# A fused decoder layer on one core: maximum rounds half a batch earlier, key products ahead of the last values, heads copied by ScalarE

## Chip, cores and metric

The kernel runs on one core of one Trainium2 chip. The metric is the device time of one execution in microseconds, the median over timed runs.

## What is computed

A pre-norm decoder layer over 16 batches of 56 tokens, 128 wide, all in float32:

```
x = x + self_attention(layernorm(x))            # 16 heads of 8, keys: the 56 tokens
x = x + cross_attention(layernorm(x), ctx, bias) # 16 heads of 8, keys: 1500 rows of ctx per batch
x = x + moe(layernorm(x))                       # 32 experts of width 64, top 4, and a shared expert
```

Cross attention is where most of the work is: keys and values are `ctx @ Wk.T` and `ctx @ Wv.T`, scores are `q.k / sqrt(8)` plus a bias per key, then softmax over 1500 keys and the weighted sum of the values. Each softmax needs the maximum over the 1500 keys, for each query and head.

## The kernel before

**Stages.** Weights and x are loaded, self attention runs over the 16 batches, then the cross attention over the 16 batches in a software pipeline of iterations (`iteration(r, c)`, batch i = 3r + c), then the router and the experts. Operands are split in two fp16 parts, and a product is three matmuls (`split_matmul`, L356 to L358). Iterations -1, 0 and 13 to 16 are written out; iterations 1 to 12 are a hardware loop of four passes over three iterations, in each engine's own program.

**One iteration** has six blocks, `for d in range(ND)`. Batch i has 12 key tiles of 125 keys, two for each block. In block d TensorE computes the scores of tile 2d (`scores`, L914) into two banks, `stb[0]` and `stb[1]`; multiplies the probabilities of the two tiles before with the values (`pv_tile`, L797 and L800); computes the scores of tile 2d + 1; then a small use of the bank `misc`, a maximum round, and a large use of `misc`. ScalarE makes each half of a score tile into probabilities (`exponential`, L1197). The two score banks are used again by the next tile, so the second half of a tile waits for the exponential of the second half of the tile before.

**Maximum rounds.** The maxima come from a second computation of the scores, without the row that subtracts the maximum: `max_round` (L891) makes eight matmuls on 31 rows and 64 columns, which fill four banks, and VectorE takes the maxima (`take_round`, L1523) in two reduces. A batch has six rounds; `round_of(d)` says which round of which batch stands in block d: rounds 2 to 5 of batch i + 1 in blocks 0 to 3, rounds 0 and 1 of batch i + 2 in blocks 4 and 5. After round 5 VectorE writes `mcol`; TensorE folds it in a small product (`mt`, L947), ScalarE copies it to `mrow` (L1217) and a DMA on ScalarE's queue (L1222) puts it into row 127 of the queries `qsb` of batch i + 1. The first scores of the next iteration wait for that DMA (`mrow_in`).

**The bank misc** is used in the order of the list `MISC`, each use waiting until the one before has been read (`misc_read`). Small uses are `sel` (block 1, `pick_heads` L807: the head sums of batch i - 1), `tr` (block 2, L944: transpose of the normalized tokens `tok`), `mt` (block 4). Large uses are V0, V1, V2 (values of batch i + 2, blocks 0 to 2) and K0, K1, K2 (keys of batch i + 3, blocks 3 to 5). After `sel`, VectorE's `normalize` (L1413 to L1419) reads misc in three operations and writes `tok`; the next large use waits for the last of them. ScalarE reads the large uses (`take_values` L1137, `take_keys` L1133).

**Other engines.** POOL splits keys (`split_keys`, L598 and L602) and the context (`split_first` L578, `split_second` L588) into two parts; SP's queue, at the start of iteration i, waits for the scores of batch i - 1 and issues for batch i + 2 two bias rows (L450), three queries (L458), three key copies (L467), then the transposes of the context of batch i + 4 (L435) and the load of that of batch i + 6 (L420). The first round of a batch waits for all of its keys and queries.

**Expert stage.** For each pair of experts and each half of the tokens TensorE makes three products of `hidden`, the `gates` product (L1003) of `pairsel` and `gt` on 64 rows, three more of `hidden`, and `down` (L1018). VectorE multiplies and splits (L1616, L1588, L1621).

## Time and profile before

| | us |
|---|---|
| median of 3 timed runs | 589.97 (588.26 to 594.99) |
| the profiled execution, device time | 591.73 |
| its span, first to last instruction | 590.0 |
| TensorE matmuls busy | 498.9 (85%) |
| VectorE busy | 383.1 (65%) |
| ScalarE busy | 333.8 (57%) |
| POOL busy | 270.5 (46%) |
| mean granted clock of TensorE | 0.901 of full speed |

L914 is line 914 of the kernel. PE is TensorE's matmul, PEld its weight load, DVE VectorE, ACT ScalarE, POOL GpSimd, SP SyncE; a q behind an engine's name is its queue. "idle before" is the time an engine stood still just ahead of the work, and behind the arrow is what ended it.

### The profile page before, as it was taken

The page shows a single profiled execution, that of the slowest core. Times are in us where ns is not written, and L with a number is a line of the kernel's source. Part 1 is how long each engine was busy: PE and PEld are TensorE (multiplying, and loading weights), DVE is VectorE, ACT ScalarE, POOL GpSimd, SP SyncE. Part 2 cuts the span into 40 slices and gives each one's busy share as a digit, 9 for nine tenths or more (in the row PEclk, how much of TensorE's full clock was granted, in tenths as well). Part 3 has the DMA queues.
Part 4 walks back from the last instruction along what each step waited for, and adds up shares of the span by engine and source line. Part 5 has one row for each costly group of instructions (what it writes and reads, how often), then busy time and mean ns, then how long its engine had stood idle before and what let it go on. Part 6 is the DMA issues. An engine that isn't in the chain of part 4 may idle for free.

```text
span 590.0 us, 17600 instructions
## 1 busy us (share of the span) xinstructions
PE 498.9 (85%) x6656; PEld 312.8 (53%) x6656; DVE 383.1 (65%) x615; ACT 333.8 (57%) x699; POOL 270.5 (46%) x201
## 2 busy tenths in 40 slices
PE   2644988768889999799979999799999887789996
PEld 1224666514556656466646656566666665334442
DVE  6972433579657767477656767477777942588885
ACT  2330165432767777477756777567776684345553
POOL 7895530074672683464570863634440040035540
PEclk9865599956789999899989999799999998599999
DMA  4147184015447547626655347516302210012101
GB/s 135 70 109 149 44 168 123 2 71 143 119 127 149 136 141 133 164 63 169 153 129 157 103 114 168 155 29 152 99 15 87 56 42 14 1 28 54 40 0 32
DMA packets 89117, 56.66 MB, mean 96 GB/s; under 512 B 74910, under 2 KB 80342, under 8 KB 89046
## 3 DMA queue, kind: packets, MB, share of 16 engines
q1 hardware_dynamic: 88390, 55.54, 37.4%
q8 instruction: 58, 0.95, 0.7%
q10 hardware_dynamic: 656, 0.06, 0.1%
q14 instruction: 13, 0.11, 0.1%
HBM read 17.01 MB, written 0.46 MB: 30 GB/s over the span
## 4 chain that ended last, share of the span: by engine, by line
PE 64%; DVE 13%; issue 10%; DMA 7%; ACT 2%; POOL 2%; SPq 1%; ACTq 0%; DVEq 0%; POOLq 0%
PE ps L914 15%; PE ps L797 10%; PE ps L356 8%; DMA qsb<-mrow 6%; PE ps L358 6%; PE ps L357 6%; DVE mx L1523 4%; PE ps L891 3%; PE ps L1018 3%; PE ps L800 3%; PE ps L773 3%; PE ps L807 2%; DVE xn L1305 2%; PE ps L1003 2%; SPq L444 1%
## 5 line engine op out<-in xcount | busy, mean ns | idle before, releaser
L1523 DVE TENSOR_REDUCE mx<-ps 120x2 f32<-120x1000 f32 x192 | 220.8, 1193 | 92.5 <-PE ps L891 92.4
L914 PE MATMUL ps<-qsb,ks 128*125 128x224 f16 x768 | 129.7, 279 | 21.6 <-issue 12.3
L1197 ACT ACTIVATE p<-ps 125x448 f32<-125x448 f32 x256 | 126.2, 540 | 31.5 <-PE ps L914 29.1
L598 POOL TENSOR_TENSOR k<-k,zero 128x500 f16<-128x500 f32 x45 | 45.9, 1020 | 142.9 <-ACT k L1133 142.9
L914 PEld LDWEIGHTS ps<-qsb,ks 128*125 128x125 f16 x768 | 78.8, 140 | 59.5 <-issue 23.7
L1197 ACT ACTIVATE wnat<-ps 125x448 f32<-125x448 f32 x128 | 63.9, 541 | 9.3 <-PE ps L914 9.2
L797 PE MATMUL ps<-p,v 125*27 125x168 f32 x1152 | 67.5, 316 | 0.4 <-DVE v L1429 0.4
L578 POOL TENSOR_TENSOR ch<-ctx,zero 128x1536 f16<-128x1536 f32 x16 | 44.9, 2807 | 23.1 <-issue 19.7
L602 POOL TENSOR_TENSOR k<-k 128x500 f16<-128x500 f32 x45 | 52.8, 1174 | 3.5
L588 POOL TENSOR_TENSOR ch<-ctx,ch 128x1536 f16<-128x1536 f32 x16 | 52.0, 3252 | 3.2 <-DMA ct<-ch 3.1
L1137 ACT ACTIVATE v<-ps 125x512 f32<-125x512 f32 x48 | 28.9, 601 | 43.3 <-PE ps L358 43.1
L891 PE MATMUL ps<-ks,qsb 31*64 31x500 f16 (+1 forms) x768 | 46.0, 417 | 4.8 <-DVE mx L1523 4.6
L356 PE MATMUL ps<-wt,ct 128*125 128x128 f16 x192 | 41.4, 246 | 5.7 <-DVE tok L1419 4.9
L669 POOL TENSOR_TENSOR ks<-ks,zero 128x384 f16<-128x384 f32 x17 | 19.6, 1155 | 51.5 <-PE ps L1018 40.2
L1133 ACT ACTIVATE k<-ps 128x500 f32<-128x500 f32 x45 | 26.4, 587 | 28.7 <-PE ps L358 28.7
L800 PE MATMUL ps<-p,v 125*9 125x56 f32 x1152 | 41.1, 215 | 0.0
L567 POOL TENSOR_TENSOR rstd<-veps,mhalf 128x4 f32<-128x4 f32 (+1 forms) x6 | 5.7, 949 | 73.3 <-DVE veps L1298 73.3
L357 PE MATMUL ps<-wt,ct 128*125 128x128 f16 x192 | 39.1, 234 | 0.0
L358 PE MATMUL ps<-wt,ct 128*125 128x128 f16 x192 | 38.9, 234 | 0.0
L356 PEld LDWEIGHTS ps<-wt,ct 128*125 128x125 f16 x192 | 28.6, 149 | 19.1 <-DVE tok L1419 8.7
L800 PEld LDWEIGHTS ps<-p,v 125*9 125x9 f32 x1152 | 32.4, 92 | 7.5
L1255 ACT ACTIVATE v<-ps 128x448 f32<-128x448 f32 x34 | 18.4, 544 | 27.5 <-PE ps L358 27.5
(184 smaller groups left out, 897.0 us busy)
## 6 DMA issues: line engine op xcount, KB each, us to landing
ks<-k SPq DMA_DIRECT2D x48, 375.0 KB
ctx<-in_ctx SPq DMA_DIRECT2D x16, 750.0 KB
ks<-in_L_ffn_W SPq DMA_DIRECT2D x48, 64.0 KB, 2.0
qsb<-late SPq DMA_DIRECT2D x32, 56.0 KB, 3.5
ks<-brow SPq DMA_DIRECT2D x32, 46.9 KB
qs<-late SPq DMA_DIRECT2D x8, 168.0 KB, 3.6
qsb<-qd SPq DMA_DIRECT2D x16, 56.0 KB, 2.6
qs<-qd SPq DMA_DIRECT2D x4, 168.0 KB, 3.8
```

The source lines that it names most:

```text
L356: nc.tensor.matmul(out, a1, b1, start=True, stop=False)
L357: nc.tensor.matmul(out, a1, b2, start=False, stop=False)
L358: return nc.tensor.matmul(out, a2, b1, start=False, stop=True)
L588: nc.gpsimd.tensor_tensor(ch[:, 1], ctx[b % 2][:], ch[:, 0], ALU.subtract).then_inc(ch_ok[1], 1)
L598: nc.gpsimd.tensor_tensor(k12[:, 0, cols], k32[:, cols], zero[:].rearrange("p a b -> p (a b)").to_broadcast([128, CH]), ALU.add).then_inc( ...
L602: nc.gpsimd.tensor_tensor(k12[:, 1, cols], k32[:, cols], k12[:, 0, cols], ALU.subtract).then_inc(k_ok, 1)
L797: mm(obank[32 * quad:32 * quad + 27, 0:168], vt[0:keys, 27 * quad:27 * quad + 27], pt[0:keys, 168 * quad:168 * quad + 168], start=first, s ...
L800: done = mm(obank[32 * quad:32 * quad + 9, 168:224], vt[0:keys, 108 + 9 * quad:117 + 9 * quad], pt[0:keys, 672 + S * quad:672 + S * quad + ...
L891: last = mm(mxb[64 * upper:64 * upper + width, j, 0:CH], qsb[n][32 * j:32 * j + 31].rearrange("p h q -> p (h q)")[:, first:first + width], ...
L914: last = mm(stb[half][0:KP, 224 * (g % 2):224 * (g % 2) + 224], ks[c % 3][:, g, KP * s:KP * s + KP], qsb[c % 3][:, HG * g:HG * g + HG].rea ...
L1197: A(p[s % 3][0:KP, 448 * half:448 * half + 448], stb[half][0:KP, 0:448], ACT.Exp, scale=SCALE).then_inc(exp_done, 1)
L1523: V.tensor_reduce(mx[:, h:h + 2, k // 2], mxb[0:120, 2 * pair:2 * pair + 2, 0:CH], axis=AX.X, op=ALU.max).then_inc(mx_read, 1)
```

## The change

Rounds 3 to 5 of batch i + 1 stand in blocks 0 to 2 and rounds 0 to 2 of batch i + 2 in blocks 3 to 5; `mt` moves to block 3 and `tr` to block 4; the keys stand in blocks 2 to 4 and V2 in block 5. Round and small use are issued ahead of the odd scores. ScalarE copies misc after `sel` to a new tile `heads`, and `normalize` reads it there, after the round. The DMA of the maximum row is issued between the two odd exponentials. SP issues keys, queries, bias rows in this order. `pairsel` and `gt` get 128 rows, the upper 64 of them zero.

```
--- before.py
+++ after.py
@@ -66,12 +66,12 @@
 
 
 
-MISC = ["V0", "sel", "V1", "tr", "V2", "K0", "mt", "K1", "K2"]
-SMALL = {1: "sel", 2: "tr", 4: "mt"}
-LARGE = ["V0", "V1", "V2", "K0", "K1", "K2"]
-
-
-TAIL = {(B - 2, "V0"): "out", (B - 2, "K0"): "norm", (B - 1, "V0"): "logits"}
+MISC = ["V0", "sel", "V1", "K0", "mt", "K1", "tr", "K2", "V2"]
+SMALL = {1: "sel", 3: "mt", 4: "tr"}
+LARGE = ["V0", "V1", "K0", "K1", "K2", "V2"]
+
+
+TAIL = {(B - 2, "V0"): "out", (B - 2, "K1"): "norm", (B - 1, "V0"): "logits"}
 OFFSET = {"K": 3, "V": 2, "s": -1, "t": -1, "m": 1}
 BEFORE_LOOP = 2 * B + 1
 
@@ -121,7 +121,7 @@
 
 def round_of(d):
 
-    return (1, d + 2) if d < 4 else (2, d - 4)
+    return (1, d + 3) if d < 3 else (2, d - 3)
 
 
 def self_uses(j):
@@ -159,7 +159,7 @@
         zero = sb("zero", [128, 1, 1], F32)
         ones_h = sb("ones_h", [128, 128], F16)
         before = sb("before", [128, 128], F16)
-        pairsel = sb("pairsel", [64, NP, 2, HE], F16)
+        pairsel = sb("pairsel", [128, NP, 2, HE], F16)
         expert_no = sb("expert_no", [128, NE], F32)
 
         wnat = sb("wnat", [128, 8, 128], F32)
@@ -214,6 +214,7 @@
         osb = sb("osb", [128, 224], F32)
         rec = sb("rec", [S, 4, 4], F32)
         tok = sb("tok", [128, D], F32)
+        heads = sb("heads", [S, 144], F32)
 
 
         flat = lambda t, d, n, o=0: t[:].rearrange("p a b -> p (a b)").bitcast(d)[:, o:o + n]
@@ -238,7 +239,7 @@
         rrec = flat(ctx[1], F32, TT, 1104)
         chosen_h = flat(ks[2], F16, 224).rearrange("p (j e) -> p j e", e=NE)
         gpair = flat(ks[2], F16, 448, 256).rearrange("p (j e) -> p j e", e=64)
-        gt = flat(ks[2], F16, T, 1024)[0:64]
+        gt = flat(ks[2], F16, T, 1024)
 
         ps = stack.enter_context(nc.psum_tensor("ps", [128, 8, 512], F32))
         sbank = [ps[:, 0:2, :], ps[:, 2:4, :]]
@@ -295,6 +296,7 @@
         misc_done = sem("misc_done")
         misc_read = sem("misc_read")
         norm_step = sem("norm_step")
+        tok_ok = sem("tok_ok")
         o_psum = sem("o_psum")
         xb_ok = sem("xb_ok")
         x_ok = sem("x_ok")
@@ -491,9 +493,9 @@
 
                 if i + 2 < B:
                     sp.wait_ge(st_done, scores_before(0, i))
+                    key_stacks(i + 2)
+                    load_queries(i + 2)
                     bias_rows(i + 2)
-                    load_queries(i + 2)
-                    key_stacks(i + 2)
                 transpose_ctx(i + 4)
                 load_ctx(i + 6)
                 if i == B - 2:
@@ -655,10 +657,9 @@
             split_first(3)
             split_second(3)
             for i in range(-1, B - 3):
-                split_keys(i + 3, 0)
+                for j in range(3):
+                    split_keys(i + 3, j)
                 split_first(i + 5)
-                split_keys(i + 3, 1)
-                split_keys(i + 3, 2)
                 split_second(i + 5)
 
             def split_experts(u, n, it):
@@ -941,6 +942,7 @@
                     pe.wait_ge(o_read, B + 3 * r + c)
                     pick_heads()
                 elif use == "tr":
+                    pe.wait_ge(tok_ok, 3 * r + c + 1)
                     tr(misc[:, 0:128], tok[:], ident[:]).then_inc(misc_done, 1)
                 elif use == "mt":
                     pe.wait_ge(mcol_ok, 3 * r + c + 2)
@@ -953,19 +955,19 @@
                     for t in (2 * d - 2, 2 * d - 1):
                         if live(r, c if t >= 0 else c - 1):
                             pv_tile(r, c if t >= 0 else c - 1, t % KT)
-                    if live(r, c):
-                        scores(r, c, 2 * d + 1)
-                    if d in SMALL:
-                        small_use(r, c, SMALL[d])
                     off, k = round_of(d)
                     if live(r, c + off):
                         max_round(r, c, off, k)
+                    if d in SMALL:
+                        small_use(r, c, SMALL[d])
+                    if live(r, c):
+                        scores(r, c, 2 * d + 1)
                     large_use(r, c, LARGE[d])
 
             for use in ("K0", "K1", "K2"):
                 large_use(0, -2, use)
             pe.wait_ge(q2_ok, 3)
-            for k in range(2):
+            for k in range(ROUNDS // 2):
                 max_round(0, -2, 2, k)
             transpose_norm(1, 1, 1, xt_psum)
             pe.wait_ge(xt2_ok, 4)
@@ -1206,9 +1208,11 @@
                     if d == 0 and live(r, c - 1):
                         act.wait_ge(pv_done, B + KT * i)
                         A(osb[:], obank[:, 0:224], ACT.Copy).then_inc(o_read, 1)
-                    if live(r, c):
-                        exponential(r, c, 2 * d + 1, 0)
                     use = SMALL.get(d)
+                    if use == "sel" and used(r, c, use):
+                        act.wait_ge(misc_done, misc_index(r, c, use) + 1)
+                        act.wait_ge(tok_ok, 3 * r + c)
+                        A(heads[:], misc[0:S, 0:144], ACT.Copy).then_inc(misc_read, 1)
                     if use == "tr" and used(r, c, use):
                         act.wait_ge(misc_done, misc_index(r, c, use) + 1)
                         A(attn[:, bass.ds(S * (i - 1), S)], misc[:, 0:S], ACT.Copy).then_inc(misc_read, 1)
@@ -1216,11 +1220,13 @@
                         act.wait_ge(misc_done, misc_index(r, c, use) + 1)
                         A(mrow[:], misc[0:H, 0:S], ACT.Copy, scale=1.0 / BIG).then_inc(misc_read, 1)
                     if live(r, c):
-                        exponential(r, c, 2 * d + 1, 1)
+                        exponential(r, c, 2 * d + 1, 0)
                     if use == "mt" and used(r, c, use):
                         act.wait_ge(misc_read, misc_index(r, c, use) + 1)
                         act.dma_start(qsb[(c + 1) % 3][MAXROW:MAXROW + 1], mrow[:]
                                       ).then_inc(mrow_in[(c + 1) % 3], 16)
+                    if live(r, c):
+                        exponential(r, c, 2 * d + 1, 1)
                     use = LARGE[d]
                     if used(r, c, use):
                         if tail(r, c, use) == "norm":
@@ -1395,8 +1401,8 @@
             for n in range(2):
                 V.memset(p[n][:], 0.0)
             V.memset(mcol[:], 0.0)
-            V.tensor_tensor(fold[:], ident[0:120, 0:S], ident[0:120, 64:120], ALU.add)
-            V.memset(tok[:], 0.0).then_inc(clear_ok, 1)
+            V.memset(tok[:], 0.0).then_inc(tok_ok, 1)
+            V.tensor_tensor(fold[:], ident[0:120, 0:S], ident[0:120, 64:120], ALU.add).then_inc(clear_ok, 1)
             self_maxima(0)
             with dve.Fori(1, B // 4, 1) as r:
                 self_maxima(r)
@@ -1406,10 +1412,10 @@
             V.tensor_tensor(xs[:], xs[:], bp[:].rearrange("p (o d) -> p o d", o=1).to_broadcast([128, TT, D]),
                             ALU.add).then_inc(xb_ok, 1)
 
-            def normalize(batches):
-
-
-                part = misc[0:S, 0:144].rearrange("p (k a e) -> p k a e", k=4, a=4)
+            def normalize(batches, src, done):
+
+
+                part = src[0:S, 0:144].rearrange("p (k a e) -> p k a e", k=4, a=4)
                 V.reciprocal(rec[:], part[:, :, :, HD]).then_inc(norm_step, 1)
                 dve.wait_ge(norm_step, batches + 1)
 
@@ -1418,7 +1424,7 @@
                                 ALU.mult)
                 V.tensor_tensor(tok[0:S, 96:128].rearrange("p (a e) -> p a e", a=4), part[:, 3, :, 0:HD],
                                 rec[:, 3, :].rearrange("p (a o) -> p a o", o=1).to_broadcast([S, 4, HD]),
-                                ALU.mult).then_inc(misc_read, 1)
+                                ALU.mult).then_inc(done, 1)
 
             def self_step(r, c):
                 j, k = 2 * r + c, c % 2
@@ -1431,7 +1437,7 @@
                                     bv[:].rearrange("p (h e) -> p h e", h=H), ALU.add).then_inc(vself_ok, 1)
                 if self_live(r, c - 2):
                     dve.wait_ge(misc_done, self_index(r, c, "sel") + 1)
-                    normalize(j - 2)
+                    normalize(j - 2, misc, misc_read)
 
                 if isinstance(r, int) and j == OUT_STEP:
                     dve.wait_ge(xb_ok, 1)
@@ -1531,12 +1537,12 @@
             def iteration(r, c):
                 i = 3 * r + c
                 for d in range(ND):
-                    if SMALL.get(d) == "sel" and used(r, c, "sel"):
-                        dve.wait_ge(misc_done, misc_index(r, c, "sel") + 1)
-                        normalize(B + i - 1)
                     off, k = round_of(d)
                     if live(r, c + off):
                         take_round(r, c, off, k)
+                    if SMALL.get(d) == "sel" and used(r, c, "sel"):
+                        dve.wait_ge(misc_read, misc_index(r, c, "sel") + 1)
+                        normalize(B + i - 1, heads, tok_ok)
                     use = LARGE[d]
                     if tail(r, c, use) == "out":
                         dve.wait_ge(misc_done, misc_index(r, c, use) + 1)
@@ -1557,7 +1563,7 @@
                     if isinstance(r, int) and i == B - 1 and 1 < d:
                         route(0, d - 1)
 
-            for k in range(2):
+            for k in range(ROUNDS // 2):
                 take_round(0, -2, 2, k)
             norm_out(1, 1, 1, xt2_ok)
             iteration(0, -1)
@@ -1605,8 +1611,9 @@
                                         gate, ALU.is_lt, ALU.mult))
             step(V.tensor_copy(gpair[:, :, 0:NE], gate))
             step(V.tensor_tensor(gpair[:, :, NE:64], gate, gpair[:, :, 0:NE], ALU.subtract))
+            V.memset(gt[64:128], 0.0)
             dve.wait_ge(gt_psum, 1)
-            V.tensor_copy(gt, ps[0:64, 5, :].bitcast(F16)[:, 0:T]).then_inc(gt_ok, 1)
+            V.tensor_copy(gt[0:64], ps[0:64, 5, :].bitcast(F16)[:, 0:T]).then_inc(gt_ok, 1)
 
             def gated(u, half):
```

## Rows read from the trace of the kernel before

**Rows 1.** The page, costliest group of VectorE (busy, mean ns, idle before)
```profile
L1523 DVE TENSOR_REDUCE mx<-ps 120x2 f32<-120x1000 f32 x192 | 220.8, 1193 | 92.5 <-PE ps L891 92.4
```

**Rows 2.** Timeline of ScalarE: line 1208, once in each iteration
```profile
440.22 0.38 ACT L1208 ACTIVATE osb<-ps 128x224 f32<-128x224 f32 x1
...
459.65 0.36 ACT L1208 ACTIVATE osb<-ps 128x224 f32<-128x224 f32 x1 [0.30 <-PE ps L800]
...
479.53 0.36 ACT L1208 ACTIVATE osb<-ps 128x224 f32<-128x224 f32 x1 [0.32 <-PE ps L800]
```

**Rows 3.** Waits: who waited for whom (us in total, times, longest)
```profile
PEld ps L914 <- ACT p L1197: 13.1, 57, 1.4
...
PE ps L914 <- DMA qsb<-mrow: 5.1, 4, 1.6
PE ps L356 <- DVE tok L1419: 4.9, 13, 0.4
```

**Rows 4.** Chain of work through one iteration (start, us, what)
```profile
380.92 0.39 PE ps L914 x4
...
394.99 0.38 PE ps L914 x4
...
398.11 0.38 PE ps L914 x4
398.49 0.42 PE ps L797 x8
...
399.39 0.34 PE ps L914 x2
...
400.14 0.34 PE ps L891 x5
400.48 0.20 PE ps L356
...
401.32 0.39 PE ps L914 x4
```

**Rows 5.** Timeline inside one block (start, us, engine, idle before)
```profile
401.36 0.60 ACT L1137 ACTIVATE v<-ps 125x512 f32<-125x512 f32 x1 [0.54 <-PE ps L358]
...
402.54 0.19 PEld L914 LDWEIGHTS ps<-qsb,ks 128*125 128x125 f16 x2
...
402.88 0.19 PEld L914 LDWEIGHTS ps<-qsb,ks 128*125 128x125 f16 x2 [0.15 <-ACT wnat L1197]
403.06 0.98 ACT L1197 ACTIVATE p<-ps 125x448 f32<-125x448 f32 x2 [0.23 <-PE ps L914]
```

**Rows 6.** Chain, then timeline, of the expert stage
```profile
538.26 0.19 PE ps L358
538.45 0.29 PE ps L1003
538.74 0.29 PE ps L356
...
541.62 0.62 DVE L1616 TENSOR_TENSOR v<-ps,v 128x448 f32<-128x448 f32 x1 [0.41 <-PE ps L358]
```

**Rows 7.** Line 1222, issue of the maximum row's DMA on ScalarE's queue
```profile
L1222 ACTq DMA_DIRECT2D qsb<-mrow x16: 510/511/589, 144.0 to 475.0; - x16
...
DMA to landing us min/median/max: 1.6/4.2/5.7
```

**Rows 8.** Timeline at a back edge of the hardware loop
```profile
240.38 0.63 PE L914 MATMUL ps<-qsb,ks 128*125 128x224 f16 x4 [3.99 <-issue]
```

**Rows 9.** Timeline of SP's queue, and landings of line 458
```profile
397.05 1.22 SPq L450 DMA_DIRECT2D ks<-brow  x2
...
401.71 2.90 SPq L467 DMA_DIRECT2D ks<-k  x3
...
DMA to landing us min/median/max: 1.9/3.5/7.4
```

**Rows 10.** Timeline of TensorE in iteration 14
```profile
467.85 0.40 PE L891 MATMUL ps<-ks,qsb 31*64 31x500 f16 x4 [0.71 <-DVE mx L1523]
```

More of the change, by code:

```diff
@@ L297, in build @@
         norm_step = sem("norm_step")
+        tok_ok = sem("tok_ok")
         o_psum = sem("o_psum")
@@ L657, in _ @@
             for i in range(-1, B - 3):
-                split_keys(i + 3, 0)
+                for j in range(3):
+                    split_keys(i + 3, j)
                 split_first(i + 5)
-                split_keys(i + 3, 1)
-                split_keys(i + 3, 2)
                 split_second(i + 5)
@@ L967, in _ @@
             pe.wait_ge(q2_ok, 3)
-            for k in range(2):
+            for k in range(ROUNDS // 2):
                 max_round(0, -2, 2, k)
@@ L1208, in iteration @@
                         A(osb[:], obank[:, 0:224], ACT.Copy).then_inc(o_read, 1)
-                    if live(r, c):
-                        exponential(r, c, 2 * d + 1, 0)
                     use = SMALL.get(d)
+                    if use == "sel" and used(r, c, use):
+                        act.wait_ge(misc_done, misc_index(r, c, use) + 1)
+                        act.wait_ge(tok_ok, 3 * r + c)
+                        A(heads[:], misc[0:S, 0:144], ACT.Copy).then_inc(misc_read, 1)
                     if use == "tr" and used(r, c, use):
@@ L1397, in _ @@
             V.memset(mcol[:], 0.0)
-            V.tensor_tensor(fold[:], ident[0:120, 0:S], ident[0:120, 64:120], ALU.add)
-            V.memset(tok[:], 0.0).then_inc(clear_ok, 1)
+            V.memset(tok[:], 0.0).then_inc(tok_ok, 1)
+            V.tensor_tensor(fold[:], ident[0:120, 0:S], ident[0:120, 64:120], ALU.add).then_inc(clear_ok, 1)
             self_maxima(0)
@@ L1407, in _, with normalize @@
                             ALU.add).then_inc(xb_ok, 1)
-            def normalize(batches):
-                part = misc[0:S, 0:144].rearrange("p (k a e) -> p k a e", k=4, a=4)
+            def normalize(batches, src, done):
+                part = src[0:S, 0:144].rearrange("p (k a e) -> p k a e", k=4, a=4)
                 V.reciprocal(rec[:], part[:, :, :, HD]).then_inc(norm_step, 1)
@@ L1533, in iteration @@
                 for d in range(ND):
-                    if SMALL.get(d) == "sel" and used(r, c, "sel"):
-                        dve.wait_ge(misc_done, misc_index(r, c, "sel") + 1)
-                        normalize(B + i - 1)
                     off, k = round_of(d)
@@ L1539, in iteration @@
                         take_round(r, c, off, k)
+                    if SMALL.get(d) == "sel" and used(r, c, "sel"):
+                        dve.wait_ge(misc_read, misc_index(r, c, "sel") + 1)
+                        normalize(B + i - 1, heads, tok_ok)
                     use = LARGE[d]
@@ L1558, in iteration @@
                         route(0, d - 1)
-            for k in range(2):
+            for k in range(ROUNDS // 2):
                 take_round(0, -2, 2, k)
```

39 lines of the change are left out of this document (22 added, 17 removed).

## The prediction

> **Forecast: 561 us, faster, range 544 to 578.** Durations are those of the one profiled execution (591.73 us, span 590.0), 1.8 us above the median of the three timed runs, 589.97. I sum the differences inside the profiled execution and take them from the median. A difference under 1% (6 us) could not be told from no change here.
>
> **What bounds the kernel now.** I began with the share of busy time. TensorE leads, and VectorE's large group is the maximum reduce, 192 times 1.193 us [rows 1]. That makes 14.3 us in an iteration of twelve reduces. The copies of line 1208, one per iteration, give the iteration's length: 19.4 and 19.9 us for iterations 13 and 14 [rows 2], and the chain from 380.92 to 401.32 gives 20.40 us for an undisturbed iteration [rows 4]. So VectorE is not the bound of the loop. The chain there is made of TensorE pieces almost alone. I call a *block* one pass of `for d in range(ND)`; there are six in an iteration. From 398.11 to 401.32, 3.21 us, a block with a value product runs: even scores 0.38, the two probability tiles 0.90 (398.49 to 399.39), odd scores 0.75 (399.39 to 400.14), round 0.34, value product 0.84 [rows 4]. The block before it, with a key product, takes 3.12 us (394.99 to 398.11). Four score matmuls take 0.38 when they are even scores and 0.75 when they are odd. The waits say why: the second half of a pair of score banks waits for the exponential that empties it, 13.1 us in 57 waits for one pair of p buffers alone [rows 3]. Inside a block [rows 5] ScalarE first takes the values out (401.36), then makes the two exponentials of the even tile, and the weight load of the odd tile's second half at 402.88 was idle 0.15 us for them. Two more waits stand on this path: the value product behind `normalize`, 4.9 us in 13 waits, or 0.38 each; and the first scores of an iteration behind the DMA of the maximum row, 5.1 us in 4 waits, one of them before the loop [rows 3].
>
> **The change part by part.**
>
> *Round ahead of odd scores.* The 0.34 us of the round now lies between the probability tiles and the odd scores. The exponentials of the even tile are then done in time, and the idle 0.15 us goes. But the same filler is missing behind the odd scores, where only the large product of 0.7 to 0.8 us is left. What is late next is ScalarE on the other side. From the weight load of the odd scores (402.54) to the start of their exponentials (403.06) are 0.52 us, the pair takes 0.98, and the next second half can load some 0.04 later, thus at +1.54 [rows 5]. Behind that come its two matmuls (0.19, half of 0.38), the tiles 0.90 and the round 0.34, to the next odd scores: 2.97 us. TensorE alone would need less, so I take this loop between the two engines as the new length of a plain block.
> Before: three value blocks of 3.21 and three key blocks of 3.12 make 18.99; of the 20.40 remain 1.41, of which 0.38 is the wait behind `normalize` and 1.03 the small products. After: 6 x 2.97 + 1.03 = 18.85.
>
> *Heads copied by ScalarE.* The bank of the small products is free after one ScalarE copy instead of three VectorE operations. The copy of 16 partitions' width of 144 columns lies in ScalarE's idle 0.23 us ahead of the odd exponentials [rows 5], or at worst delays them: its cost is between 0 and 0.36 us (the 224 column copy of line 1208 [rows 2]); I take 0, the copy being smaller than the slot and the scores of 0.38 us standing between it and its reader. If that cover were gone the price is 16 x 0.36 = 5.8 us at most. The wait of 0.38 us goes, as counted. `normalize` moves behind the round on VectorE; what waits for it is the transpose three blocks later, so nothing is behind it. The added `tok_ok` wait of the copy is for the transpose's data of the batch before, long done; behind it on ScalarE stand the odd exponentials, and the same wait on TensorE has the odd scores behind it.
>
> *The DMA issue of the maximum row.* It moves ahead of the second odd exponential. The issue occupies ScalarE's queue 0.51 us [rows 7] where the next exponential would have followed after about 0.45 (half of the pair's 0.98 less overlap). The exponential is on the loop just described. Its cost lies between 0 and 0.51 us; I take 0.2, the excess after overlap. The iteration becomes 19.05, which is 1.35 less. For the twelve iterations in the hardware loop: 16.2 us. Iteration 0 has no small products of a batch before it: 0.5.
>
> *Maxima half a batch ahead.* The row's DMA leaves in block 3 instead of 4. Between its product and the next iteration's first scores lie then the rest of block 3 (some 1.5 us) and two blocks, 7.4 us, against a landing of 1.6 to 5.7 us [rows 7]. So the four waits go: 5.1 us [rows 3]. The first of these, 1.7 us, is spent again: before iteration 0 stand nine rounds instead of eight, and there VectorE takes 2 x 1.193 = 2.4 us a round. Part of that is hidden behind the first row's DMA; I give back 1.7 us. Net 3.4. At the three back edges of the loop TensorE stands still for up to 3.99 us, put down to issue and not to data [rows 8]. I leave these as they are; that the earlier row shortens them is bounded by 0 and 1 us each.
>
> *Tail.* In iteration 14 four rounds, the addition to x and the layer norm meet on VectorE, and TensorE waits for its reads, 0.71 us in one place [rows 10]. One round of 2.4 us leaves it for iteration 13, where VectorE has room. I take 2.0 us for iteration 14, bounded by 0 and 2.4, and 0.7 for iteration 13, half of 1.35, as its key products are missing.
>
> *Keys ahead of values; SP's order.* The products only change places. SP issues two bias rows, three queries, three key copies from 397.05 to 404.61, 7.6 us, in either order [rows 9]. Iteration 11 began at 398.11, so the last is issued at +6.5. Batch i+2 is wanted by its first round in block 3 instead of 4: three blocks and the small products and 1.3 us into block 3, at about +10.8. With the median landing of 3.5 us that is 0.8 us early. Cost 0, between 0 and what the second rival says. POOL's three key splits stand together and the context's first part behind them, some two blocks earlier than it is needed: 0.
>
> *Gates on 128 rows.* The gate product's matmul takes 0.29 and its successor 0.29, where the neighbours take 0.19 [rows 6]: 0.20 us lost around each of 32 products of 64 rows. With all operands on 128 rows the two switches go: 6.4 us. VectorE has 0.41 us idle in each half unit of 2.1 us [rows 6], so it doesn't take over at 1.9. The added memset of `gt` stands where VectorE waits for transposes: 0, and 0.62 us (an operation of 448 columns [rows 6]) if not hidden. The Trainium skill, TensorEngine Tiling (Array Packing), section Tiling Modes, says that changing the mode drains the engine, not changing the tile; its section on performance considerations, though, names row tiling as what to use for a contraction of 64 rows or fewer, which speaks against this edit. By the second the edit would gain nothing or lose; a single product with nothing beside it bears out the first, and the trace agrees with it in these two pieces of 0.29.
>
> Sum: 16.2 + 0.5 + 3.4 + 2.0 + 0.7 + 6.4 = 29.2, so 589.97 - 29.2 = 560.8, **561 us**.
>
> **The rivals.**
> *A, no new wait on ScalarE (15%).* The round and the odd scores fit so that TensorE alone counts. A block is then 0.38 + 0.90 + 0.34 + 0.48 (odd scores at the price of the even ones and 0.10 for a switch, as at the gates [rows 6]) + product 0.74 or 0.65 (each 0.10 less, as it has no switch ahead of it any more): 2.84 or 2.75, an iteration 16.77 + 1.03 + 0.2 = 18.0. That is 1.05 less than the forecast's, over 14 iterations 15: 546 us. For it: modelled ends may overstate the 0.52. Against: the waits of rows 5 are real and only moved.
> *B, the waits only change sides (17%).* What the odd scores win the even ones lose, so a block stays at 3.1 to 3.2. Then of 1.35 only 0.38 less 0.2 is left, and 14 x 1.1 = 15 us are missing: 576 us.
> *C, keys late, slower (6%).* The last of batch i+2's DMAs lands after its first round wants it. TensorE stops in block 3 of each iteration with a batch to come, 14 times. With the longest landing seen, 7.4 us [rows 9], it lands at +13.9, 3.1 us late, 43 us in all: 604 us. It costs more than the gain from 29.2 / 14 = 2.1 us of lateness, a landing of 6.4 us. Against: the median is 3.5, and bias rows are small. The Trainium skill, DMA: Bandwidth & Descriptors, section Issuing engines are not separate DMA queues, says that DMAs from all engines share the same 16 and interleave. The trace agrees: the maximum row of 1.8 KB lands in 1.6 us alone and in 5.7 at worst [rows 7].
> *D, the maxima do not get ahead (4%).* VectorE runs late after `normalize`, and the product of `mcol` waits for it with the odd scores behind it. At half a reduce, 0.6 us, in 15 iterations it costs 9 us: 570 us.
>
> **How the numbers follow.** The forecast has 58%. Its own terms move by 6 us either way. The range 544 to 578 takes in A, B and D with a margin of 2 us, and leaves out C and the far ends, some 2 in 10. Faster by over 1% is all but C and the part of B and the forecast in which more than one term fails: 0.89. Within 1%: 0.05. Slower by over 1%: 0.06.
>
> **What would show it.** Undisturbed iterations at 19.0 us between copies of `osb` (18.0 speaks for A, 20 for B); the wait for `tok` ahead of the value product gone; score waits on ScalarE in even rather than odd tiles; no wait for `mrow` outside back edges; the three back edges still near 4 us; the gate and its successor at 0.19 and the expert stage 6 us shorter. Wrong if TensorE waits for a DMA of keys or queries at the first round, or if iterations keep 20.4 us.

## The result, and the profile after

The changed kernel takes 594.09 us (median of 20 runs, 591.38 to 596.08); beside it the kernel before took 591.08 (20 runs). The ratio is 1.0049, with a 95% interval of 1.0029 to 1.0068: a loss of half a per cent, where 561 us and a clear gain had been forecast. The profiled execution spans 594.2 us instead of 590.0.

From the page of the changed kernel (last number of the q1 row: time of its packets as a share of the 16 DMA engines; line numbers are one to seven above those of before):

```profile
span 594.2 us, 17674 instructions
...
PEclk9865599855599998799989999899999989599998
...
q1 hardware_dynamic: 88390, 55.54, 43.2%
q8 instruction: 58, 0.95, 0.7%
...
L1529 DVE TENSOR_REDUCE mx<-ps 120x2 f32<-120x1000 f32 x192 | 221.1, 1195 | 102.5 <-PE ps L892 102.4
...
L915 PEld LDWEIGHTS ps<-qsb,ks 128*125 128x125 f16 x768 | 79.9, 142 | 73.1 <-ACT p L1199 35.8
```

VectorE's reduces are what they were [rows 1]. TensorE's mean granted clock is 0.885 instead of 0.901. And the same 88390 packets and 55.54 MB of q1 now take 43.2% of the DMA engines' time, where the page of before has 37.4%: the same bytes are longer under way. The packets of the queue that the page calls instruction take 0.7%, as before.

The copies of `osb`, one per iteration, from the timeline of ScalarE:

```profile
195.76 0.36 ACT L1210 ACTIVATE osb<-ps 128x224 f32<-128x224 f32 x1
...
216.72 0.36 ACT L1210 ACTIVATE osb<-ps 128x224 f32<-128x224 f32 x1
...
244.55 0.36 ACT L1210 ACTIVATE osb<-ps 128x224 f32<-128x224 f32 x1 [0.67 <-PE ps L801]
...
267.45 0.36 ACT L1210 ACTIVATE osb<-ps 128x224 f32<-128x224 f32 x1
...
404.48 0.36 ACT L1210 ACTIVATE osb<-ps 128x224 f32<-128x224 f32 x1
...
424.51 0.36 ACT L1210 ACTIVATE osb<-ps 128x224 f32<-128x224 f32 x1
```

An undisturbed iteration (404.48 to 424.51) takes 20.03 us, which answers to the 20.40 of [rows 4]. From copy to copy the two such iterations of before took 20.33 and 20.34, those of the changed kernel 20.03 and 19.84. So the chain is a little faster, by 0.3 to 0.5 us, not by 1.35. Iterations that have a back edge (the jump to the start of the hardware loop), and those behind one, are much slower. From 216.72 to 244.55 are 27.83 us, where the iteration before the change took 25.09 (217.63 to 242.72), and the next takes 22.90 instead of 20.95. The waits, one pair of p buffers in the second row (us in total, times, longest):

```profile
POOL k L600 <- DMA ks<-brow: 47.5, 8, 7.5
...
PEld ps L915 <- ACT p L1199: 35.8, 112, 2.5
...
PE ps L915 <- issue: 13.9, 4, 4.9
```

The second half-loads of the scores now wait for ScalarE 112 times and 35.8 us, where [rows 3] had 57 times and 13.1. POOL waits for the bias rows of the next batch, 8 times up to 7.5 us, a wait that the kernel before doesn't have. In all POOL stands still ahead of this line about as long as before (139.9 and 142.9 us), so the wait matters as a sign of late data more than as a cost.

SP's queue in iteration 3, then what POOL and TensorE stood still for at that time, and TensorE in iteration 10 (timelines):

```profile
215.19 1.90 SPq L469 DMA_DIRECT2D ks<-k  x3
...
219.57 1.20 SPq L452 DMA_DIRECT2D ks<-brow  x2
220.88 10.82 SPq L437 DMA_TRANSPOSE ct<-ch  x2
...
228.48 1.02 POOL L600 TENSOR_TENSOR k<-k,zero 128x500 f16<-128x500 f32 x1 [7.46 <-DMA ks<-brow]
...
228.55 0.22 PE L801 MATMUL ps<-p,v 125*9 125x56 f32 x2 [2.37 <-issue]
...
389.82 0.39 PE L892 MATMUL ps<-ks,qsb 31*64 31x500 f16 x2
391.28 0.41 PE L892 MATMUL ps<-ks,qsb 31*64 31x500 f16 x6 [1.07 <-issue]
```

SP goes through keys, queries and bias rows from 215.19 to 220.77 and starts the transposes at once. The bias rows are issued at 219.57 and land at 228.48, where POOL is let go: 8.9 us, against 3.5 in the median and 7.4 at most for the queries before [rows 9] (for the bias rows of before, for which nobody waited, no landing is on the page). TensorE stands still at the same moment, for 2.37 us put down to issue (the profile shows nothing that it waited for), in the middle of the matmuls of one probability tile, where the program has no wait. In iteration 10 it stands still for 1.07 us behind the second matmul of a round, where there is none either.

### The profile page after: what moved, and what is told of

Same layout as the page of the kernel before. It is cut to its first block, busy times and chain, and to the rows that moved or that the text cites. A ratio compares the mean times of both kernels' runs of the same rounds, so it can differ in the third digit from the quotient of the medians.

```text
span 594.2 us, 17674 instructions
## 1 busy us (share of the span) xinstructions
PE 496.0 (83%) x6656; PEld 317.8 (53%) x6656; DVE 393.0 (66%) x616; ACT 335.1 (56%) x715; POOL 269.9 (45%) x201
## 3 DMA queue, kind: packets, MB, share of 16 engines
q1 hardware_dynamic: 88390, 55.54, 43.2%
## 4 chain that ended last, share of the span: by engine, by line
PE 57%; issue 14%; DVE 14%; ACT 7%; DMA 3%; SPq 2%; POOL 2%; DVEq 1%; ACTq 0%; POOLq 0%
PE ps L915 15%; PE ps L798 11%; PE ps L892 6%; PE ps L358 4%; PE ps L359 4%; PE ps L360 4%; DVE mx L1529 3%; PE ps L801 3%; ACT p L1199 3%; DVE v L1628 3%; PE ps L774 3%; ACT v L1269 3%; PE ps L808 2%; DVE xn L1311 2%; SPq L446 2%
## 5 line engine op out<-in xcount | busy, mean ns | idle before, releaser
L915 PE MATMUL ps<-qsb,ks 128*125 128x224 f16 x768 | 134.4, 283 | 26.3 <-issue 13.9
L1199 ACT ACTIVATE p<-ps 125x448 f32<-125x448 f32 x256 | 127.5, 547 | 31.7 <-PE ps L915 27.8
L915 PEld LDWEIGHTS ps<-qsb,ks 128*125 128x125 f16 x768 | 79.9, 142 | 73.1 <-ACT p L1199 35.8
L600 POOL TENSOR_TENSOR k<-k,zero 128x500 f16<-128x500 f32 x45 | 45.9, 1020 | 139.9 <-ACT k L1135 92.4
L798 PE MATMUL ps<-p,v 125*27 125x168 f32 x1152 | 68.3, 319 | 0.4 <-DVE v L1435 0.4
L590 POOL TENSOR_TENSOR ch<-ctx,ch 128x1536 f16<-128x1536 f32 x16 | 53.7, 3359 | 4.1 <-DMA ct<-ch 3.0
L580 POOL TENSOR_TENSOR ch<-ctx,zero 128x1536 f16<-128x1536 f32 x16 | 45.2, 2822 | 22.9 <-issue 19.7
L892 PE MATMUL ps<-ks,qsb 31*64 31x500 f16 (+1 forms) x768 | 47.8, 424 | 6.9 <-DVE mx L1529 3.4
L604 POOL TENSOR_TENSOR k<-k 128x500 f16<-128x500 f32 x45 | 51.1, 1136 | 3.5
L358 PE MATMUL ps<-wt,ct 128*125 128x128 f16 x192 | 39.2, 236 | 0.0
L359 PE MATMUL ps<-wt,ct 128*125 128x128 f16 x192 | 38.3, 232 | 0.0
L360 PE MATMUL ps<-wt,ct 128*125 128x128 f16 x192 | 38.3, 232 | 0.0
L670 POOL TENSOR_TENSOR ks<-ks,zero 128x384 f16<-128x384 f32 x17 | 14.1, 827 | 53.4 <-PE ps L1020 40.5
L774 PE MATMUL ps<-ks,qs 96*112 (+1 forms) x128 | 18.5, 284 | 17.5 <-DMA qs<-qd 16.4
L798 PE MATMUL ps<-wnat,v 125*27 125x168 f32 x512 | 31.8, 320 | 0.4 <-ACT wnat L1199 0.4
```

Of the source, the lines that this page charges most:

```text
L358: nc.tensor.matmul(out, a1, b1, start=True, stop=False)
L359: nc.tensor.matmul(out, a1, b2, start=False, stop=False)
L360: return nc.tensor.matmul(out, a2, b1, start=False, stop=True)
L590: nc.gpsimd.tensor_tensor(ch[:, 1], ctx[b % 2][:], ch[:, 0], ALU.subtract).then_inc(ch_ok[1], 1)
L600: nc.gpsimd.tensor_tensor(k12[:, 0, cols], k32[:, cols], zero[:].rearrange("p a b -> p (a b)").to_broadcast([128, CH]), ALU.add).then_inc( ...
L604: nc.gpsimd.tensor_tensor(k12[:, 1, cols], k32[:, cols], k12[:, 0, cols], ALU.subtract).then_inc(k_ok, 1)
```

## The experiments

All but one start from the changed kernel. Their times have the kernel before, run beside them, at 589.6 to 591.9 us, so ratios are compared; the 95% interval of a kernel with four runs is 3 to 5 us to either side.

**1. SP's old order.**

```
-                    key_stacks(i + 2)
-                    load_queries(i + 2)
                     bias_rows(i + 2)
+                    load_queries(i + 2)
+                    key_stacks(i + 2)
```

> The changed kernel with SP's old order alone (bias rows, queries, key copies last). Theory Q (the queue's order took the gain: key copies in flight just where TensorE jumps back in its loop and where queries, bias rows and transposes follow): the back edges fall from 3.8 to 4.9 us to 3.3 to 4.0, the stalls put down to issue inside blocks (2.4, 1.5, 1.1, 0.8 us) go, and the time falls by 8 to 12 us against the changed kernel, to 582 to 586. Rival S (ScalarE is what took the gain): the time stays within 2 us of the changed kernel, 594, and so do the stalls.

Measured: 580.1 us, ratio 0.983 (0.975 to 0.991), some 14 us less than the changed kernel (13 by the ratios) and 2 us below what was expected. Experiments 2 and 9 are a second pair that differs in SP's order alone: ratios 1.005 and 0.982, again 13 to 14 us. Two copies of `osb`, from ScalarE's timeline:

```profile
193.07 0.36 ACT L1210 ACTIVATE osb<-ps 128x224 f32<-128x224 f32 x1
...
212.94 0.36 ACT L1210 ACTIVATE osb<-ps 128x224 f32<-128x224 f32 x1
```

The iteration takes 19.87 us, and so do all that have no back edge at or just before them. The stalls inside blocks are gone, POOL waits for no bias rows, and the packets of q1 take 36.7% instead of 43.2%. One half of the expectation failed: the gaps at the three back edges are 4.5 to 4.9 us, no shorter than with the keys first (3.8 to 4.9) and longer than before [rows 8]. So it is not the back edge itself that the order makes longer.

**2. The maximum row's DMA issued last.**

```
+                    if live(r, c):
+                        exponential(r, c, 2 * d + 1, 1)
                     if use == "mt" and used(r, c, use):
...
                         act.dma_start(qsb[(c + 1) % 3][MAXROW:MAXROW + 1], mrow[:]
                                       ).then_inc(mrow_in[(c + 1) % 3], 16)
-                    if live(r, c):
-                        exponential(r, c, 2 * d + 1, 1)
```

> The changed kernel with the DMA of the maximum row issued behind both odd exponentials, as before. Theory S: in the trace of the changed kernel the two exponentials of block 3 start 0.64 us apart instead of 0.43, and the block takes 3.6 us instead of 3.0 to 3.1; undone, each iteration wins 0.3 to 0.5 us, 5 to 8 us in all, 586 to 589. Theory Q: at most 2 us.

Measured: 592.25 us, ratio 1.0048 (1.0006 to 1.009), not told apart from the changed kernel. An undisturbed iteration takes 19.80 or 19.63 us instead of 20.03 and 19.84: the issue costs 0.2 us, as the prediction had it, and not 0.3 to 0.5. In all that is 3 us, and with the keys first it is lost in the stalls. The stalls put down to issue are at the same instructions again. In the timeline of this kernel, iterations 4 and 10:

```profile
251.81 0.41 PE L892 MATMUL ps<-ks,qsb 31*64 31x500 f16 x6 [1.06 <-issue]
...
388.61 0.41 PE L892 MATMUL ps<-ks,qsb 31*64 31x500 f16 x6 [1.07 <-issue]
```

**3. Gates on 64 rows.** `pairsel` and `gt` as before, the memset out.

> The changed kernel with the gate product back on 64 rows and without the memset. If the edit won the 2 us that the traces show between the two expert stages (4.08 instead of 4.20 us for a unit of two halves), this is 1 to 3 us slower than the changed kernel, 595 to 597, and VectorE's second part lasts 0.62 us in both halves again instead of 1.10 in one of them. If the prediction was right about 6.4 us, it is 600.

Measured: 594.76 us, ratio 1.0107 (1.0032 to 1.0181). Against the changed kernel's 1.0049 that is in the expected direction, but within the intervals. The stages say more: from the first gate product to the last copy are 68.3 us with 64 rows, as before the change, and 66.2 with 128. The second part of VectorE and the weight split of POOL in this kernel (each line's duration in ns, least, median, most):

```profile
L1594 DVE TENSOR_TENSOR v<-v x34: 615/616/673, 513.9 to 585.6; 128x448 f16<-128x448 f32 x34
...
L670 POOL TENSOR_TENSOR ks<-ks,zero x17: 825/1298/1298, 478.2 to 571.3; 128x384 f16<-128x384 f32 x17
```

**4. Odd scores first again.** On TensorE `scores(r, c, 2 * d + 1)` stands ahead of the round and the small product, on ScalarE the first odd exponential ahead of the small copies.

> The changed kernel with the odd scores ahead of the round and the small product on TensorE, and the first odd exponential ahead of the small copies on ScalarE. Theory S in its strong form (the round in front only moved the wait to the other side): the same time within 2 us as the changed kernel. The prediction's step (a plain block falls from 3.2 to 3.0): 3 to 6 us slower, 597 to 600, with odd waits back. Theory Q says nothing of it: the stalls on issue stay.

Measured: 606.42 us, ratio 1.031 (1.023 to 1.039), 12 us slower than the changed kernel, where the prediction's step had let expect 3 to 6. Two copies of `osb`:

```profile
410.88 0.37 ACT L1210 ACTIVATE osb<-ps 128x224 f32<-128x224 f32 x1
...
432.15 0.38 ACT L1210 ACTIVATE osb<-ps 128x224 f32<-128x224 f32 x1
```

21.27 us: without the new order the rest of the change makes an iteration 0.9 us longer than it was before the change. So the order is worth 1.2 to 1.4 us in an iteration, and the strong form of the rival (the wait only changes sides) falls. The stalls on issue did not stay as expected: one of 1.21 us is left, in the round of block 0 of iteration 10, and none in iterations 3 and 9, though the keys go first.

**5. Where the keys may go first.** The old order, but `if i in (4, 7, 10)` the new one.

> The changed kernel with SP's old order, except in iterations 4, 7 and 10, where the key copies go first as in the change: these are the iterations that TensorE enters over a back edge of its loop. If the harm of the order comes from instructions that cannot be fetched at the back edge, nearly all of the 14 us come back, 590 to 594. If it comes from what the order does inside a block (queries, bias rows and transposes behind the keys), three of thirteen iterations carry it: iterations 4, 7 and 10 take 22.9, 21.6 and 22.1 us as in the changed kernel against 20.4, 20.1 and 21.1 with the old order, 5 us in all, 584 to 586.

Measured: 586.77 us, ratio 0.9945 (0.991 to 0.998), close to the second reading (584 to 586) and below the first. Iterations 4, 7 and 10 take 22.37, 22.55 and 23.03 us against 20.38, 20.08 and 21.13 with the old order throughout: 6.4 us in three iterations. Busy time in stretches behind the second and third back edges (PE, PEld, DVE, ACT, POOL, then granted clock, DMA share, GB/s), first with the old order, from the first scores of the iteration and 3 us on, then 3 us behind the third edge:

```profile
301.60:304.60 3.00, 2.94 (x44) 1.85 (x44) 0.00 (x0) 1.20 (x3) 1.09 (x1) 0.50 0.68 252
304.60:307.60 3.00, 2.91 (x60) 2.17 (x52) 2.31 (x2) 2.29 (x6) 0.00 (x0) 0.98 1.00 197
...
370.00:373.00 3.00, 3.00 (x28) 2.69 (x20) 2.31 (x2) 1.58 (x5) 0.00 (x0) 0.50 1.07 247
```

and with the keys first, 3 and 6 us behind the first scores at the same two edges:

```profile
307.80:310.80 3.00, 2.61 (x25) 2.06 (x18) 2.31 (x2) 1.23 (x3) 0.00 (x0) 0.50 1.33 60
310.80:313.80 3.00, 3.00 (x50) 1.89 (x48) 0.07 (x1) 1.47 (x3) 0.00 (x0) 0.58 0.58 92
...
375.20:378.20 3.00, 2.40 (x23) 1.87 (x16) 2.31 (x2) 1.20 (x3) 0.00 (x0) 0.50 1.33 61
378.20:381.20 3.00, 3.00 (x48) 1.90 (x46) 0.00 (x0) 1.47 (x3) 0.00 (x0) 0.50 0.57 88
```

Behind a back edge the clock is at its lower level, 1.2 GHz, 0.50 in the row. From 3 us on TensorE is busy without a gap or nearly so with the old order (2.91 to 3.00 of 3 us), and has idle time with the keys first (2.33 to 2.61). That holds at all three edges. The clock differs from edge to edge. At the second, the row 3 us on shows 0.98 with the old order; with the keys first it is 0.50, then 0.58. At the third it is still 0.50 with the old order too, and only the row behind it is back at 1.00, where the keys first have 0.50 once more. At the first edge the two orders are alike (0.79 and 0.81). In the changed kernel it is other edges again: 3 us on the clock is 0.50 at the first, 0.83 at the second and 0.93 at the third. So the keys first bring idle time behind a back edge, and at some edges a longer time at the lower level, but which edges varies between runs; that the idle time is the reason is not shown.

**6. Transposes held** until the keys, queries and bias rows just issued have landed:

```
+                    if i > 0:
+                        sp.wait_ge(*keys_in(0, i + 2))
+                        sp.wait_ge(*queries_in(0, i + 2))
```

> The changed kernel, keys first, but SP holds the transposes of the context until the keys, queries and bias rows just issued have landed. Theory T (the transposes, issued right behind the bias rows, hold up everything small behind them, TensorE's instructions too): bias rows land by 9 us into the iteration instead of 11 to 12.4, the in-block stalls put down to issue (2.4, 1.5, 1.1, 0.8) are gone, 580 to 585. Rival K (the key copies alone do it): bias rows and stalls stay as they are, 592 to 596.

Measured: 590.11 us, ratio 0.998 (0.994 to 1.002). Between the two. Bias rows still land late: in iteration 3 they are issued at 219.07 and POOL is let go at 226.81, 7.7 us later, with no transpose issued between 210.9 and 226.7. TensorE waits 0.85 us for them once. So the key copies ahead of them are enough to make them late. But the stalls on issue inside blocks are gone, and iterations 2, 3 and 9 come down to 19.9, 26.0 and 25.8 us, from 21.0, 27.8 and 27.4. Those behind back edges stay at 21.6, 22.9 and 22.7.

**7. POOL's split shifted,** together with the edits of 1 and 2: `pool.wait_ge(u2_ok, 2 * (u - NW) + 4)` ahead of it.

> SP's old order, the maximum row's DMA behind both odd exponentials, and in the expert stage POOL's weight split starts only when VectorE has finished the second part that it now runs into. Theory P (POOL and VectorE are in each other's way, and who starts first wins): VectorE's second part takes 0.62 us in both halves again, a unit 3.8 us instead of 4.08, 4 us in all. With the DMA's 0.2 us in each of 15 iterations, 572 to 575. Without an effect of the shift: 577 to 579.

Measured: 580.24 us, ratio 0.984 (0.975 to 0.992). That is above both expected ranges. The shift did nothing of what it was made for: the expert stage takes 67.3 us instead of 65.7, and VectorE's second part still lasts up to 1.29 us. It now runs into the second of POOL's two operations.

**8. Heads from the bank,** with the edit of 1: VectorE reads `misc` again, ahead of its reduces; ScalarE's copy is out.

> SP's old order, and the heads not copied: VectorE normalizes from the bank itself, ahead of its reduces of the round, as before the change. The prediction's step: the value product of block 1 waits 0.4 us more, 5 to 6 us in all, 585 to 587. If the odd scores that now stand between the small product and the value product cover the wait, the copy is worth nothing, 579 to 582.

Measured: 582.52 us, ratio 0.986 (0.979 to 0.993), between the two expectations. An undisturbed iteration takes 20.0 to 20.2 us (one 20.35) instead of 19.85. The copy wins 0.2 to 0.3 us and not 0.38. Over 16 iterations that would be 3 to 5 us; the two times are 2.4 us apart, within their intervals. The scores between the two products cover part of the wait.

**9. Edits 1 and 2 together.**

> The changed kernel with SP's old order and the maximum row's DMA behind both odd exponentials. Plain iterations of 19.64 us as in the run with the shifted weight split, the expert stage 66 us as with the old order alone (the shift is out again): 577 to 579, 2.2% faster than before. If the DMA's place doesn't matter, 580 to 581.

Measured: 578.83 us, ratio 0.982 (0.978 to 0.985). Undisturbed iterations take 19.64 us.

**10. A quarter of POOL's weight split,** on top of 9. From the fourth pair on, 32 of each 128 columns are split; the others keep the values of earlier experts, so this kernel doesn't compute the layer and serves to measure alone.

> The same kernel, with POOL's split of the expert weights done for a quarter of the columns only from the fourth pair of experts on (the other columns keep the values of earlier experts). Theory P: POOL's operations shrink to a fraction, VectorE's second part takes 0.62 us everywhere, a unit of two halves 3.8 us instead of 4.08, the stage 3.5 to 4.5 us shorter than in the kernel beside it, 573 to 575. If VectorE's own work is the bound, the stage keeps its length within 1 us.

Measured: 574.14 us, ratio 0.975 (0.970 to 0.980). The chain of this kernel, two gate products in a row:

```profile
535.16 0.19 PE ps L1006
...
537.05 0.19 PE ps L1006
```

1.89 us for half a unit, with TensorE alone on the chain, where the changed kernel needs 2.04. The stage is 62.1 us long instead of 65.7.

**11. The order alone,** on the kernel before: round and small product ahead of the odd scores, small copies ahead of the odd exponentials, nothing else of the change.

> The kernel before, with one part of the change alone: round and small product ahead of the odd scores on TensorE, the small copies ahead of both odd exponentials on ScalarE. The maxima, the keys and the heads stay as they were. If this part carries the gain of the loop, an undisturbed iteration takes 19.9 to 20.1 us instead of 20.34, the waits for the maximum row's DMA stay or grow (one block less between its product and the scores is not given back), 584 to 588. If the parts only work together, 589 to 593.

Measured: 585.5 us, ratio 0.995 (0.991 to 0.999). Iterations without a back edge that don't wait for the maximum row take 19.84 to 19.91 us, as those of the whole change do. The waits for the row grow: 2.11, 1.03, 2.08, 1.10 and 1.02 us, where [rows 3] had 5.1 us in 4.

**12. First part of the weights by ScalarE,** on top of 9, from the fourth pair on:

```
+                    A(wh[m][:, 0], wf[m][:], ACT.Copy).then_inc(wh_step, 1)
```

> SP's old order, the maximum row's DMA last, and the first part of each pair's weights copied to fp16 by ScalarE (from the fourth pair on), where it stands idle between its two kinds of work; POOL only subtracts. Theory P: with one of POOL's two operations gone, VectorE's second part meets it less, a unit of two halves takes 3.8 to 3.9 us instead of 4.08, the stage 2.5 to 4 us less: 574 to 576, 2.5% faster than before. If the 0.45 us copy on ScalarE delays the silu behind it instead, the unit stays at 4.1 or grows: 578 to 581.

Measured: 574.17 us, ratio 0.972 (0.969 to 0.975). It is faster than both kernels. Timeline of the expert stage:

```profile
541.43 0.51 ACT L1287 ACTIVATE ks<-ks 128x384 f16<-128x384 f32 x1
...
541.65 0.62 DVE L1609 TENSOR_TENSOR v<-v 128x448 f16<-128x448 f32 x1
...
542.01 1.03 POOL L674 TENSOR_TENSOR ks<-ks 128x384 f16<-128x384 f32 x1 [2.76 <-ACT ks L1287]
```

The copy of 0.51 us follows the work before it on ScalarE without a gap, POOL has one operation per unit, and VectorE's second part lasts 0.62 us each time. The stage is 62.1 us long.

## Why the prediction was wrong, point by point

**SP's order: the step that failed.** "The products only change places. SP issues ... in either order" was priced at 0. It cost 13 to 14 us, as experiment 1 and the pair of 2 and 9 show, and turned a gain of 1.7% into a loss. The prediction counted SP's issue time, which is the same, and bounded the landing by the worst of before. It did not ask what the key copies, 1.1 MB with the small transfers queued behind them, do to everything else that comes by DMA. Before, bias rows and queries went out first, and only the transposes, for which POOL waited 3.1 us in the whole kernel, stood behind the keys. Rival C had the right row to look at (a landing of 7.4 us and more) and the right direction, but its mechanism is small: at a round TensorE waited for the queries once, 1.04 us in iteration 2, and never for the keys. The rest came as stalls inside runs of matmuls that have no wait, as a wait for ScalarE behind a back edge (1.1 us once), and in part as clock (0.885 against 0.901 in experiment 1). From copy to copy of `osb`, against experiment 1, the changed kernel loses 5.5 us in iterations 2, 3 and 9, of which experiment 6 gives back 4.5 by holding the transposes; 5.0 us in the three iterations behind back edges (6.4 in experiment 5); and 1.2 us in the others. Another 2.7 us lie ahead of the first copy, but these can't be put down to the order: the first copy comes at 170.7 to 174.9 us in experiments 7, 9, 10 and 12, which have the same code up to there, and at 172.9 in experiments 2 and 3, which have the keys first.

That the stalls are instructions that had not arrived is an inference. For it: they stand in no iteration but those with the keys first; the profile puts them down to issue; and over four runs (the changed kernel and experiments 2, 3 and 5) they stand at the same places of the program: behind the second matmul of the round in block 2 of one to three of iterations 4, 7 and 10, and in three of these runs inside the same `pv_tile` of iterations 3 and 9. Against it: experiment 4 has the keys first, and its one stall stands elsewhere; the 58 packets of the instruction queue take no larger share of the DMA engines' time with the keys first (0.7%, and 0.8% in experiment 1), though a delay ahead of a packet would not show in that; and with the transposes held (experiment 6) they are gone, though the keys still go first, so the key copies alone don't bring them. No run took the fetches themselves away, so this was not tried.

**Round ahead of odd scores: right mechanism, size off.** The waits moved to the even scores, as said, and TensorE and ScalarE close the loop described. The chain of the changed kernel through blocks 2 to 4:

```profile
411.55 0.53 PE ps L915 x4
...
412.71 0.29 PE ps L915 x2
...
413.03 0.41 PE ps L915 x2
413.44 0.42 PE ps L798 x8
...
414.45 0.41 PE ps L892 x6
...
415.07 0.35 PE ps L915 x2
...
415.52 0.54 ACT p L1199
...
416.16 0.55 ACT p L1199
...
416.76 0.41 PE ps L915 x2
...
418.41 0.26 PE ps L946
```

From the odd scores (411.55) to the first probability tile (413.44) are 1.89 us; the prediction had 1.54 and 0.19. The mis-sized term is the 0.19: the second half, once it has waited, takes 0.41 until the tiles start, and not half of 0.38. The trace of before already had this figure, at the second half of the odd scores (the row below). Why the two matmuls then take 0.41 is not shown. With 0.90 and 0.34 a plain block is 3.13 us, not 2.97. From 415.07 to 418.41 the DMA's issue stands between the exponentials (415.52 and 416.16, 0.64 apart), and costs the 0.2 that was taken. Experiment 2 bears out the issue's price, experiment 4 the order. The gain of an iteration was 0.5 us instead of 1.35. What the prediction missed most is that two effects met: without the new order the rest of the change costs 0.9 us an iteration (experiment 4), and with the new order alone the old kernel already reaches 19.9 (experiment 11). Beside the order the other parts nearly cancel in an undisturbed iteration: the heads win 0.2 to 0.3 (experiment 8), the DMA's place costs 0.2 (experiment 2). The half batch serves against the waits for the row.

```profile
399.73 0.41 PE ps L914 x2
```

*Back edges.* The prediction left them as they were, or up to 1 us shorter. With the old SP order TensorE stands still there for 4.5, 4.9 and 4.5 us, where it stood 4.0, 3.7 and 3.3 before: 2.8 us lost in all. The order alone has 3.2, 4.0 and 4.1 (experiment 11). Why they grow stays open.

**Maxima half a batch ahead: right.** No `mrow` wait is left in the changed kernel or in experiment 1. Experiment 11 shows what they would have grown to with the faster blocks, 7.3 us in all. The time up to the first copy of `osb` was 2.2 us shorter with the old SP order, 0.5 forecast; with a spread of 4 us from run to run this says nothing of the half batch.

**Heads: right, and smaller.** 0.2 to 0.3 us each, not 0.38 (experiment 8).

**Gates on 128 rows: right cause, a third of the size.** The gate and its neighbours now follow each other at 0.19 (experiment 10's chain; the matmuls at 545.33 and 545.52 in the fence below are the gate's and the one after it). The Trainium skill, TensorEngine Tiling (Array Packing), section Tiling Modes, says that TensorE drains when the mode changes; the trace agrees, with 0.29 us each for the gate product and its successor on 64 rows [rows 6] and 0.19 on 128. But "VectorE has 0.41 us idle, so it doesn't take over" was wrong. The changed kernel, one half unit:

```profile
545.01 0.83 POOL L670 TENSOR_TENSOR ks<-ks,zero 128x384 f16<-128x384 f32 x1 [2.00 <-PE ps L1020]
...
545.22 1.10 DVE L1594 TENSOR_TENSOR v<-v 128x448 f16<-128x448 f32 x1
545.33 0.35 PE L1005 MATMUL ps<-ks,pairsel 128*128 128x448 f16 x1
...
545.52 0.35 PE L358 MATMUL ps<-xt,ks 128*128 128x448 f16 x1
...
546.37 0.30 PEld L1020 LDWEIGHTS ps<-v,ks 128*128 128x128 f16 x3 [0.56 <-DVE v L1594]
```

POOL's split starts 0.21 us ahead of VectorE's second part, which then lasts 0.5 us longer than alone, and the down product waits 0.56 us for it. With 64 rows both start at the same time, and POOL pays: VectorE's part takes 0.62 us and POOL's 1.30 (experiment 3). In experiment 12 VectorE is 0.36 us ahead, takes 0.62, and POOL's operation 1.03 instead of 0.91. The Trainium skill, GPSIMD Engine Reference, section Specifications, says that GpSimd and VectorE share their way to SBUF and get in each other's way where a VectorE instruction has two SBUF inputs. The trace agrees: L1594, with two, goes from 0.62 to 1.10 us, and L1628, with one input from PSUM, stays at 0.61 to 0.63 while POOL works. The edit won 2.1 us and not 6.4; experiments 10 and 12 give 3.6 more by taking work off POOL.

**Tail: wrong.** Forecast 2.7 us for iterations 13 and 14, measured 0.1 in the first and a loss of 0.7 in the second with the old SP order, and 0.5 lost in iteration 15. Experiment 11, which leaves the rounds where they were, loses the same: 20.51 us in iteration 14 and 16.18 in 15, against 20.56 and 16.19 in experiment 1 and 19.88 and 15.64 before. So the loss comes with the order of rounds and scores, and the round taken out of iteration 14 gave nothing. The 1.4 us of waits for the maxima went, but TensorE now waits 1.2 us for `mcol` there, which is rival D's mechanism in one iteration, and more for ScalarE.

Together, with the old SP order: 7.5 us from iterations 1 to 12 and 2.6 from the experts, less 1.1 at the tail, make 9 us of the 29 forecast, or 11 with the 2.2 ahead of iteration 1 that may be chance; and the queue's order took 13 to 14. So even with SP's step at the 0 that it was given the time would have been 580 us (experiment 1), at the upper edge of the range and far from 561.

## What to carry to other kernels

When a DMA queue's order changes, ask not only when the moved transfers land, but what else needs a DMA while the large ones fly: small transfers that someone waits for go out first, large ones whose reader is far last. A wait taken off one side of a loop between two engines turns up on the other; work out the whole loop, with the time that a half takes after it has waited. And an engine's idle time may be no room if another engine works on SBUF at that moment (POOL and VectorE here): see how long its operations last when they overlap.

## What the hardware showed that was not expected

TensorE stood still for up to 2.4 us (2.7 in experiments 2 and 3) inside runs of independent matmuls while SBUF to SBUF key copies and transposes had just been issued, at the same places of the hardware loop's body in four runs. POOL's split and VectorE's second part, both reading and writing SBUF, slow each other: 0.83 and 1.10 us with POOL ahead by 0.2, 1.30 and 0.62 with both starting together.
